# Cross-attention and soft mixture of experts: dispatch with an identity, token-major attention, another order in both stages

## The chip, the cores and the metric

The program runs on one core of a Trainium2 chip. The metric is the device time of one execution, in microseconds (us). TensorE multiplies (its products land in PSUM, eight banks of 512 float32 per partition), VectorE and ScalarE move and change data, GpSimd does plain tensor work, SyncE issues most transfers. Each engine works through its own list in order; semaphores join the lists.

## The reference, cut to what matters

```python
# x (32, 64, 256): 2048 tokens, 16 tiles of 128 tokens (2 sequences each); ctx (32, 64, 128)
q = layernorm(x) @ Wq; k, v = split(ctx @ Wkv)           # 32 heads of 8
q, k = rope(q, pos), rope(k, pos)
w = softmax(q . k / sqrt(8))                              # per head, 64 x 64
x = x + (w @ v) @ Wout + bout
xl = layernorm(layernorm(x)) * gamma + beta               # 16 experts, 128 slots each
logits = l2norm(xl) * scale . l2norm(mu)                  # token x 2048
dispatch = softmax over tokens; combine = softmax over the 2048 slots
slot_in = dispatch^T @ xl                                 # per sequence
h = gelu(slot_in @ W1 + b1)                               # 64 hidden
x = x + combine @ (h @ W2 + b2)
```

## The kernel before, in words

Everything stays in SBUF; a tile is 128 tokens. The first stage walks the 16 tiles through attention, the second through the experts. Both are software pipelines whose order is written out by hand, engine by engine: a `step(s)` of the first stage does the softmax of tile s, the rotary embedding of s + 1, the transposes of s + 2, the attend of s - 1 and the output projection of s - 2. Matmuls that want more than float32r precision are split in a high and a low part (`mm3`, lines 915 to 917, three passes). A plain float32 product is two passes in the profile, a transpose one.

First stage. TensorE projects q, k and v (`project_qk`, `project_v`), transposes q and k (`transpose_kq`, lines 948 to 951), forms the logits of the 32 heads in banks 0 to 3, with k masked by head so that pieces of 32 rows by 64 columns can be used (`logits`, line 965), transposes p (line 980), and attends (line 994). The attend has v as stationary operand, so the output comes transposed, and a second set of products with a matrix of ones, `hone`, gives the sums of p, repeated for each of the 8 dimensions of a head. VectorE takes maxima and subtracts (lines 677, 682), multiplies by cosine and sine (654, 656) into `ra` and `rb`, adds them (664), masks half of k (672), adds the residual and takes its statistics (702, 704), and divides (694, 696). ScalarE exponentiates (462), copies p transposed (466), v (479), q (483) and the other half of k (488), and casts x (493). GpSimd normalises x (347 to 353), and prepares mu, W1 and W2 with 2048-wide operations (378 to 407). The norms of mu's columns are summed on TensorE in steps 3 to 6 (1024) and spread over the partitions by a product of ones with a diagonal matrix between steps 7 and 8 (1085, 523).

Second stage, a tile: `expand` (xl @ W1, 12 passes), `transpose_e` (1127), the transposes of the next xl (1097), `dispatch` (1140), `slot_logits` of the next tile (24 passes of 512 columns), `combine` (1148, 1155) and `contract` (1161 and 24 passes of 256 columns). Dispatch computes e^T @ (xl @ W1), per expert, with both sequences of a tile in one product of 128 rows: the right side holds 65 columns for each sequence, with zeros in the other sequence's rows, and a column of ones that sums e over tokens. VectorE divides by that sum (842, 844), and ScalarE applies gelu (551). The exponent is line 539, the finish of a tile line 861.

## Time and profile before

| | us |
|---|---|
| median of 3 runs (range) | 567.08 (566.81 to 567.75) |
| span of the profiled execution | 560.9 |
| TensorE, VectorE, ScalarE, GpSimd busy | 501.4, 422.3, 290.3, 148.5 |
| second softmax starts | 37.94 |
| first, last finish of a tile in the second stage | 268.7, 558.1 |

The span runs from the first to the last instruction of one execution; the profile gives no other time for that execution, and the runs' median is 6.2 us above the span. A busy share is an average over both stages. The weight loads (PEld) overlap the passes (PE). The timelines count from the span's start; the end of a pass is modelled, so the rate of passes is best read from one start to the next.

### The profile page before, as it was taken

The numbers are of one execution on the slowest core, as the hardware profiler recorded it, in microseconds if no ns is written. First come the engines' busy times: TensorE is split into PE (matmuls) and PEld (weight loads), VectorE is DVE, ScalarE is ACT, GpSimd is POOL, SyncE is SP. The second block draws the span as 40 slices with busy tenths as digits, with TensorE's granted clock in tenths as the row PEclk, the third lists the DMA queues.
The fourth block names the chain that finished last, engine by engine and source line by source line (L and its number), as shares of the span: only waits on it lengthen the run. The fifth ranks groups of instructions, "written<-read, shape, count | busy, mean of one in ns | idle before, by whom it ended". The sixth has DMA issues, their size and how long they took to land.

```text
span 560.9 us, 14312 instructions
## 1 busy us (share of the span) xinstructions
PE 501.4 (89%) x5544; PEld 406.3 (72%) x5544; DVE 422.3 (75%) x823; ACT 290.3 (52%) x537; POOL 148.5 (26%) x248
## 2 busy tenths in 40 slices
PE   0676999987797878889999999999999999999997
PEld 0444666654565555668888898898889889888986
DVE  5788998896799999856866686686668668666854
ACT  1363656664354646635455635745563574556344
POOL 4329211518363832311211212111121211112100
PEclk9868999999698989999999999999999999999999
DMA  6500000006000200000000000000000000000000
GB/s 188 197 6 6 8 6 7 8 1 160 6 6 5 62 0 1 4 1 1 11 11 2 11 9 9 0 9 9 0 9 9 9 0 9 9 0 9 11 11 11
DMA packets 15665, 11.65 MB, mean 21 GB/s; under 512 B 7040, under 2 KB 15120, under 8 KB 15376
## 3 DMA queue, kind: packets, MB, share of 16 engines
q1 hardware_dynamic: 15632, 11.18, 6.7%
q8 instruction: 25, 0.41, 0.3%
q14 instruction: 8, 0.07, 0.0%
HBM read 9.08 MB, written 2.10 MB: 20 GB/s over the span
## 4 chain that ended last, share of the span: by engine, by line
PE 75%; DVE 16%; ACT 3%; issue 2%; SPq 1%; DMA 1%; POOL 0%; DVEq 0%; ACTq 0%
PE bank L915 13%; PE bank L917 12%; PE bank L916 12%; PE bank L1140 10%; PE bank L1155 6%; PE bank L1127 5%; DVE qkr L664 4%; PE bank L965 4%; PE bank L980 4%; PE bank L994 3%; DVE rc L694 3%; PE bank L1014 2%; DVE mx L677 2%; PE bank L1161 2%; DVE pb L682 2%
## 5 line engine op out<-in xcount | busy, mean ns | idle before, releaser
L462 ACT ACTIVATE pb<-pb 128x512 f32<-128x512 f32 x64 | 39.4, 632 | 64.2 <-DVE pb L682 64.2
L545 ACT COPY mu_raw<-bank 128x512 f32<-128x512 f32 x34 | 19.7, 588 | 98.4 <-PE bank L1127 98.4
L1140 PE MATMUL bank<-w_raw,eb 128*128 128x130 f32 x512 | 60.2, 275 | 1.0 <-DVE w_raw L815 0.9
L1140 PEld LDWEIGHTS bank<-w_raw,eb 128*128 128x128 f32 x512 | 58.5, 190 | 1.5 <-DVE w_raw L815 1.4
L551 ACT ACTIVATE pb<-pb 128x768 f32<-128x768 f32 (+1 forms) x48 | 37.1, 774 | 40.1 <-DVE pb L844 40.1
L915 PE MATMUL bank<-mun_h,xlT_l 128*128 128x512 f32 x128 | 51.9, 405 | 0.2 <-DVE xlT_l L806 0.2
L844 DVE TENSOR_TENSOR pb<-bank,rh 128x384 f32<-128x384 f32 x96 | 49.3, 513 | 3.3
L980 PEld LDWEIGHTS bank<-ident,pb 128*128 128x128 f32 x256 | 31.3, 156 | 27.7 <-issue 25.0
L980 PE MATMUL bank<-ident,pb 128*128 128x128 f32 x256 | 45.9, 309 | 5.8 <-ACT vb L479 3.6
L917 PE MATMUL bank<-mun_h,xlT_h 128*128 128x512 f32 x128 | 50.6, 395 | 0.0
L916 PE MATMUL bank<-mun_l,xlT_h 128*128 128x512 f32 x128 | 50.5, 395 | 0.0
L815 DVE TENSOR_TENSOR w_raw<-bank,mu_raw 64x512 f32<-64x512 f32 x64 | 44.1, 689 | 6.4 <-PE bank L917 4.9
L677 DVE TENSOR_REDUCE mx<-bank 128x8 f32<-128x512 f32 x64 | 41.0, 682 | 9.3 <-PE bank L965 9.2
L539 ACT ACTIVATE eb<-bank,nshift,rn 128x512 f32<-128x512 f32 x64 | 44.9, 777 | 3.2 <-PE bank L917 1.6
L965 PE MATMUL bank<-kT,qT 32*64 32x256 f32 x512 | 45.1, 443 | 0.0
L854 DVE TENSOR_TENSOR gT_l<-bank,gT_h 128x512 fp32r<-128x512 f32 x32 | 22.1, 692 | 26.8 <-ACT gT_h L556 26.8
L420 POOL TENSOR_TENSOR xc<-xc,mu_raw 128x256 f32<-128x256 f32 x16 | 11.8, 735 | 115.0 <-DVE xc L792 115.0
L334 POOL TENSOR_TENSOR sm<-sm,mhalf 128x1 f32<-128x1 f32 x16 | 8.8, 549 | 123.6 <-DVE sm L799 123.6
L682 DVE TENSOR_TENSOR pb<-bank,mx 128x512 f32<-128x512 f32 x64 | 40.9, 679 | 0.0
L466 ACT COPY pT<-bank 128x512 f32<-128x512 f32 x64 | 35.7, 594 | 7.9 <-PE bank L980 7.7
L850 DVE COPY esT<-bank 16x128 f32<-16x128 f32 x16 | 4.4, 278 | 45.8 <-PE bank L1148 45.8
L915 PE MATMUL bank<-w_h,gT_l 128*128 128x256 f32 x128 | 37.1, 290 | 0.0
(156 smaller groups left out, 1261.2 us busy)
## 6 DMA issues: line engine op xcount, KB each, us to landing
mu_raw<-in_L_ffn_mu SPq DMA_DIRECT2D x1, 2048.0 KB, 12.8
out<-w_raw SPq DMA_DIRECT2D x16, 128.0 KB, 1.7
xa<-in_x SPq DMA_DIRECT2D x1, 1536.0 KB, 8.4
ctile<-in_ctx SPq DMA_DIRECT2D x16, 64.0 KB, 1.9
w_raw<-in_L_ffn_W SPq DMA_DIRECT2D x2, 512.0 KB, 5.3
w_raw<-in_L_ffn_W SPq DMA_DIRECT2D x1, 1024.0 KB, 9.1
xa<-in_x SPq DMA_DIRECT2D x1, 512.0 KB, 3.6
mu_raw<-in_L_ffn_b SPq DMA_DIRECT2D x1, 512.0 KB, 3.1
```

The lines of the kernel that those rows point to most:

```text
L462: a.activation(pb[:, p, gr], pb[:, p, gr], ACT.Exp, scale=HD ** -0.5).then_inc(p_ready, 1)
L539: a.activation(eb[:, 4 * c:4 * c + 4, :].rearrange("p a b -> p (a b)"), bank[LB[c]][:], ACT.Exp, scale=rn[:, p:p + 1], bias=nshift[:]).the ...
L677: v.reduce_max(mx[:, gr, :], bank[gr][:].rearrange("p (h k) -> p h k", k=SEQ), AX.X)\
L682: v.tensor_tensor(pb[:, p, gr], bank[gr][:].rearrange("p (h k) -> p h k", k=SEQ), mx[:, gr, :].unsqueeze(2).broadcast_to([P, 8, SEQ]), ALU ...
L815: v.tensor_tensor(xw[rows, 8 * c:8 * c + 8, b * HC:b * HC + HID], bank[2 + c][rows].rearrange("p (e h) -> p e h", h=HID), b1b[rows, 8 * c: ...
L844: v.tensor_tensor(hb[:, e0:e0 + n], src[:, :, :, 0:HID], rh[:, e0:e0 + n, :].unsqueeze(3).broadcast_to([P, n, 2, HID]), ALU.mult).then_inc ...
L915: mm(o, a[1], b[0], start=first, stop=False)
L916: mm(o, a[0], b[1], start=False, stop=False)
L917: return mm(o, a[0], b[0], start=False, stop=last)
L965: m = mm(bank[g][cols, 256 * half:256 * half + 256].rearrange("p (j n) -> p j n", j=4), qT[rows, half, cols], kT[rows, half, :, cols], sta ...
L980: m = nc.tensor.transpose(bank[6 + gr % 2][:, i * P:(i + 1) * P], pb[:, p, gr, 2 * i:2 * i + 2, :].rearrange("p h k -> p (h k)"), ident[:])
L1140: m = mm(bank[HB[i % 3]][:, n * 2 * HC:(n + 1) * 2 * HC], eb[:, e, :], xw[:, e, :], start=True, stop=True)
```

## The change

In words, for what the diff below leaves out as well:

- Second stage: each expert's dispatch is two products, one for each sequence, on 64 rows each and into two neighbouring banks. Their right side is xl @ W1 + b1 and the ones (65 columns) beside a 64 x 64 identity, so that columns 65 to 128 hold e transposed; `transpose_e` is gone. ScalarE copies those columns to eT for each group of three experts, and only then VectorE divides that group. `xw_copy` adds b1 for both sequences at once. b2 and the sums of e are split in three float32r parts, and one pass replaces the float32 product. expand of s + 1 and the transposes of s + 2 come ahead of contract of s. The sums of e are taken a bank at a time. The LN statistics of later tiles move from the first stage into tiles 0, 4 and 8 of the second.
- First stage: the attend has p transposed as stationary operand and v as moving one, with 2 columns of ones for the sums, so the output is token-major with 32 sums; it is divided (`on`), transposed on TensorE (`transpose_o`) and copied by ScalarE (`oT`). The sine product stays in the bank, q, k and all transposes of tile s + 1 share bank 4, six scaled copies of k are ScalarE's and two heads' copies are VectorE's. The logits of all four row groups come together. The steps of TensorE and ScalarE are written out instead of looped over.
- mu's inverse norms go to DRAM and come back spread over the partitions by a transfer, and GpSimd reads them with a stride.
- Start: x of tile 0 has its own transfer and is normalised by VectorE; the weights are on ScalarE's queue; dummy transposes of the identity stand in TensorE's list.

```diff
+XC = HC + SEQ
+VC = 2 * HD + 2
...
+vb = sb("vb", P, 3, 2, HEADS // 2, VC)
...
-PER = BANK // (2 * HC)
+PER = BANK // XC
 HG = [range(i, min(i + PER, EXPERTS)) for i in range(0, EXPERTS, PER)]
 GG = [(HG[i][0], HG[min(i + 1, len(HG) - 1)][-1] + 1) for i in range(0, len(HG), 2)]
-NB = (6, 7, 5, 6)
-LB = (0, 1, 2, 5)
-HB = (4, 5, 3)
+LB = (2, 3, 0, 1)
+HB = (6, 0, 4)
...
+def pair(i, n):
+    b0 = HB[i % 3]
+    return psum[:, b0:b0 + 2, 0:n * XC].rearrange("p b (n c) -> p b n c", c=XC)
...
-    sp.dma_start(xa[:, 0:AHEAD, :], x_d[:, 0:AHEAD, :]).then_inc(x_loaded[0], 16)
+    sp.dma_start(xa[:, 0, :], x_d[:, 0, :]).then_inc(x_loaded[0], 16)
     load_ctx(0, 0)
-    sp.dma_start(wqkv_raw[:, 0:KD, :], Wq.rearrange("(k p) n -> p k n", p=P)).then_inc(wqkv_loaded, 16)
-    sp.dma_start(wqkv_raw[:, KD:KD + 2, :], Wkv.rearrange("p (k n) -> p k n", k=2)).then_inc(wqkv_loaded, 16)
-    sp.dma_start(posb[:], pos_d).then_inc(pos_loaded, 16)
+    sp.dma_start(xa[:, 1:AHEAD, :], x_d[:, 1:AHEAD, :]).then_inc(x_loaded[1], 16)
+    load_ctx(1, 1)
+    sp.wait_ge(wqkv_loaded, 32)
...
             load_ctx(i * 2 + p, p)
-    sp.wait_ge(rb_filled, 4)
+    load_ctx(10, 0)
+    sp.wait_ge(mur_ready, 1)
+    sp.dma_start(mur_d, mu_r[:, 1, :]).then_inc(mur_stored, 16)
+    sp.wait_ge(mur_stored, 16)
+    sp.dma_start(mu_rb, row(mur_d.rearrange("s e -> (s e)"), ES)).then_inc(rb_loaded, 16)
+    load_ctx(11, 1)
...
+        mu_k = mu_raw[:, k, :].rearrange("p (e s) -> p e s", s=SLOTS)
+        g.tensor_tensor(mu_k, mu_k, mu_rb.rearrange("p (s e) -> p e s", e=EXPERTS), ALU.mult)\
+            .then_inc(muscale_step, 1)
...
+    a.dma_start(posb[:], pos_d).then_inc(pos_loaded, 16)
+    a.dma_start(wqkv_raw[:, 0:KD, :], Wq.rearrange("(k p) n -> p k n", p=P)).then_inc(wqkv_loaded, 16)
+    a.dma_start(wqkv_raw[:, KD:KD + 2, :], Wkv.rearrange("p (k n) -> p k n", k=2)).then_inc(wqkv_loaded, 16)
...
+    def k1_copy(t, b=4, b0=4):
+        for half, j in ((1, 0), (1, 1), (1, 2), (1, 3), (0, 2), (0, 3)):
+            src = bank[b][:, DIM:DIM + P] if half else bank[b0][:, DIM + P:DIM + 2 * P]
+            a.activation(kT[:, half, j, :], src, ACT.Copy, scale=hmask[:, j:j + 1]).then_inc(k1_ready, 1)
...
+    def oT_copy(t):
+        act.wait_ge(oT_filled, t + 1)
+        wait(act, a_filled, t)
+        a.copy(oT[:], bank[5][:, 0:DIM]).then_inc(oT_ready, 1)
+    def step(s, p, before=True, after=True, out=True, ahead=True):
+        if before:
+            for gr in range(2):
+                pT_copy(s - 1, gr)
+        for gr in range(2):
+            exp_group(s, p, gr)
+        if out:
+            oT_copy(s - 2)
+        if before:
+            for gr in range(2, GROUPS):
+                pT_copy(s - 1, gr)
         if after:
-            v_copy(s + 1, 1 - p)
+            v_copy(s + 1)
             q_copy(s + 1)
+            k1_copy(s + 1)
             if ahead:
-                xT_high(s + 2)
-            k1_copy(s + 1)
-    act.wait_ge(consts_dve, 4)
-    xT_high(0)
...
+    def eT_copy(t):
+        for i, gr in enumerate(HG):
+            n, e0 = len(gr), gr[0]
+            act.wait_ge(h_filled, t * len(HG) + i + 1)
+            a.copy(eT[:, e0:e0 + n, :].rearrange("p n (b k) -> p b n k", b=2),
+                   pair(i, n)[:, :, :, HC:XC]).then_inc(eT_ready, 1)
...
-        v.tensor_tensor(rb[:], src, sinb[:, t, :].unsqueeze(1).broadcast_to([P, 64, 8]), ALU.mult)\
+        v.tensor_tensor(src, src, sinb[:, t, :].unsqueeze(1).broadcast_to([P, 64, 8]), ALU.mult)\
             .then_inc(ropeab_done, 1)
...
         dve.wait_ge(ropeab_done, t * 2 + 2)
+        rb = bank[4][:].rearrange("p (h c e) -> p (h c) e", c=4, e=2)
         for e in range(2):
             v.tensor_tensor(qkr[:].rearrange("p a (n e) -> p (a n) e", e=2)[:, :, e],
                             ra[:].rearrange("p h (c e) -> p (h c) e", e=2)[:, :, e],
-                            rb[:].rearrange("p h (c e) -> p (h c) e", e=2)[:, :, 1 - e],
+                            rb[:, :, 1 - e],
                             ALU.add).then_inc(qk_roped, 1)
...
-    def normalise(t):
+    def normalise(t, b=5):
         dve.wait_ge(o_filled, t + 1)
-        v.reciprocal(rc[:], bank[4][:, DIM:2 * DIM]).then_inc(rc_done, 1)
+        src = bank[b][:, 0:HEADS // 2 * VC].rearrange("p (q c) -> p q c", c=VC)
+        v.reciprocal(rc[:].rearrange("p (q j) -> p q j", j=2), src[:, :, 2 * HD:VC]).then_inc(rc_done, 1)
         dve.wait_ge(rc_done, t + 1)
-        v.tensor_tensor(oT[:], bank[4][:, 0:DIM], rc[:], ALU.mult).then_inc(oT_ready, 1)
...
+    def step(s, p, before=True, after=True, out=True, ahead=True, norms=False, stats=False):
         softmax(s, p, 0)
         if after:
             rope_products(s + 1)
+            rope_sums(s + 1)
+        if out:
+            residual(s - 2, stats=stats)
         if norms:
             dve.wait_ge(muss_ready, 1)
-            v.tensor_scalar(mu_r[:, 0, :], bank[5][:, DIM:DIM + EXPERTS], L2_EPS * L2_EPS, None, ALU.max)\
+            v.tensor_scalar(mu_r[:, 0, :], bank[5][:, BANK - EXPERTS:BANK], L2_EPS * L2_EPS, None, ALU.max)\
                 .then_inc(muss_clamped, 1)
         softmax(s, p, 2)
         if after:
-            rope_sums(s + 1)
-        if out:
-            residual(s - 2)
-        if after:
             k0_copy(s + 1)
-        if ahead:
-            xT_low(s + 2)
         if before:
             normalise(s - 1)
+        if ahead:
+            xT_low(s + 2, p)
...
+    def slot_sums(t, chunks=range(4)):
+        for c in chunks:
+            dve.wait_ge(e_ready, t * 4 + c + 1)
+            v.reduce_sum(es[:, 4 * c:4 * c + 4], eb[:, 4 * c:4 * c + 4, :], AX.X).then_inc(es_ready, 1)
...
+    def hidden(t):
         for i, gr in enumerate(HG):
-            if i == 3 and not last:
-                eT_copy(t, 3)
             n, e0 = len(gr), gr[0]
-            dve.wait_ge(h_filled, t * len(HG) + i + 1)
-            src = bank[HB[i % 3]][:, 0:n * 2 * HC].rearrange("p (n b c) -> p n b c", b=2, c=HC)
-            v.reciprocal(rh[:, e0:e0 + n, :], src[:, :, :, HID]).then_inc(rh_done, 1)
+            dve.wait_ge(eT_ready, t * len(HG) + i + 1)
+            src = pair(i, n)
+            v.reciprocal(rh[:, :, e0:e0 + n], src[:, :, :, HID]).then_inc(rh_done, 1)
             dve.wait_ge(rh_done, t * len(HG) + i + 1)
-            v.tensor_tensor(hb[:, e0:e0 + n], src[:, :, :, 0:HID],
-                            rh[:, e0:e0 + n, :].unsqueeze(3).broadcast_to([P, n, 2, HID]),
+            v.tensor_tensor(hb[:, e0:e0 + n].rearrange("p n b h -> p b n h"), src[:, :, :, 0:HID],
+                            rh[:, :, e0:e0 + n].unsqueeze(3).broadcast_to([P, 2, n, HID]),
                             ALU.mult).then_inc(hn_ready, 1)
...
             clamp(s + 1, 1 - p)
-        xw_copy(s)
-        if not last:
-            xlT_copy(s + 1)
-        hidden(s, last)
-        if not last:
-            eT_copy(s, 1)
+        hidden(s)
         if ahead:
             center(s + 2, p)
+        if stats:
+            batch_stats(stats)
+        if not last:
+            slot_sums(s + 1)
+        esT_copy(s)
         gT_low(s)
         if not last:
+            xw_copy(s + 1)
             sums(s + 1, 1 - p)
+        if ahead:
+            xlT_copy(s + 2)
         finish(s, p)
...
+    def keep_busy(n):
+        for _ in range(n):
+            nc.tensor.transpose(bank[5][:, 0:P], ident[:], ident[:])
...
+    def logits(t):
+        pe.wait_ge(q_ready, t + 1)
+        pe.wait_ge(k1_ready, t * 6 + 6)
+        pe.wait_ge(k0_ready, t + 1)
         wait(pe, sub_done, t * 4)
-        nc.tensor.transpose(bank[2][:, 0:P], qkr[:, 1, 0:P], ident[:]).then_inc(kq_filled, 1)
-        for k in range(KD):
-            nc.tensor.transpose(bank[3][:, k * P:(k + 1) * P], qkr[:, 0, k * P:(k + 1) * P], ident[:])
-        nc.tensor.transpose(bank[3][:, DIM:DIM + P], qkr[:, 1, P:2 * P], ident[:]).then_inc(kq_filled, 1)
...
-                if half and b:
-                    m.then_inc(s_filled, 1)
+        for half in range(2):
+            for b in range(2):
+                for g in range(GROUPS):
+                    rows, cols = slice(32 * g, 32 * g + 32), slice(64 * b, 64 * b + 64)
+                    m = mm(bank[g][cols, 256 * half:256 * half + 256].rearrange("p (j n) -> p j n", j=4),
+                           qT[rows, half, cols], kT[rows, half, :, cols], start=True, stop=True)
+                    if half and b:
+                        m.then_inc(s_filled, 1)
...
+    def attend(t, bo=5):
...
+        for q in range(HEADS // 2):
+            i = 4 * (q % 8 // 2) + 2 * (q // 8) + q % 2
             for b in range(2):
-                for r in range(2):
-                    for g in range(GROUPS):
-                        c = 256 * r + 32 * (half * GROUPS + g)
-                        product(half, r, g, vb[:, p, b].rearrange("p r c -> p (r c)")[:, c:c + 32],
-                                slice(64 * b, 64 * b + 64), half * P + b * 64)
-            for r in range(2):
-                for g in range(GROUPS):
-                    m = product(half, r, g, hone[:, r, :], slice(0, P), DIM + half * P)
+                rows = slice(64 * b, 64 * b + 64)
+                m = mm(bank[bo][rows, q * VC:(q + 1) * VC], pT[:, i, rows], vb[:, t % 3, b, q, :],
+                       start=True, stop=True)
         m.then_inc(o_filled, 1)
+    def transpose_o(t):
+        pe.wait_ge(on_ready, t + 1)
+        wait(pe, x1_ready, t)
+        for k in range(KD):
+            m = nc.tensor.transpose(bank[5][:, k * P:(k + 1) * P], on[:, k * P:(k + 1) * P], ident[:])
+        m.then_inc(oT_filled, 1)
...
-        if before:
-            transpose_p(s - 1, 1 - p, 1, more=after)
-        logits(s, 0, 1)
-        if before:
-            transpose_p(s - 1, 1 - p, 2)
+            for gr in range(2):
+                transpose_p(s - 1, 1 - p, gr, more=after)
         if after and before:
-            project_qk(s + 1)
-        logits(s, 2, 0)
+            project_qk(s + 1, 1 - p)
         if norms is not None:
             mu_sums(s, norms)
+        if out:
+            transpose_o(s - 2)
         if before:
-            transpose_p(s - 1, 1 - p, 3)
-        logits(s, 2, 1)
-        if norms == 3:
-            pe.wait_ge(muss_clamped, 1)
+            for gr in range(2, GROUPS):
+                transpose_p(s - 1, 1 - p, gr)
         if out:
             for k in range(KD):
                 project_out(s - 2, k)
         if after:
-            project_v(s + 1)
-            if before:
-                attend(s - 1, 1 - p)
+            project_v(s + 1, 1 - p)
             transpose_kq(s + 1)
             if ahead:
                 transpose_x(s + 2, p)
+        if norms == 3:
+            pe.wait_ge(muss_clamped, 1)
+        if before:
+            attend(s - 1, 5 if after else 4)
+    keep_busy(24)
     transpose_x(0, 0)
+    keep_busy(8)
     pe.wait_ge(wqkv_ready, 1)
-    project_qk(0)
-    project_v(0)
+    project_qk(0, 0)
+    project_v(0, 0)
+    keep_busy(6)
     transpose_x(1, 1)
-    transpose_kq(0)
-    project_qk(1)
+    transpose_kq(0, 3, 2)
+    project_qk(1, 1)
...
+    def dispatch(t, last, first=False):
+        pe.wait_ge(xw_ready, t * 2 + 2)
         for i, gr in enumerate(HG):
-            if i == 0:
+            if i == 1:
+                pe.wait_ge(e_ready, t * 4 + 4)
+                if not last:
+                    pe.wait_ge(xlT_ready, t + 2)
+            if i == 2:
                 wait(pe, yo_ready, t)
+                if first:
+                    pe.wait_ge(x1_ready, TILES)
             if i >= 3:
                 pe.wait_ge(hn_ready, t * len(HG) + i - 2)
             for n, e in enumerate(gr):
-                m = mm(bank[HB[i % 3]][:, n * 2 * HC:(n + 1) * 2 * HC], eb[:, e, :], xw[:, e, :],
-                       start=True, stop=True)
+                for b in range(2):
+                    rows = slice(64 * b, 64 * b + 64)
+                    m = mm(bank[HB[i % 3] + b][:, n * XC:(n + 1) * XC], eb[rows, e, :], xw[rows, e, :],
+                           start=True, stop=True)
             m.then_inc(h_filled, 1)
...
+    def ffn_step(s, p, last=False, ahead=True, first=False):
+        dispatch(s, last, first)
         if not last:
             slot_logits(s + 1)
-        combine(s, last)
+        combine(s)
+        if not last:
+            expand(s + 1)
+        if ahead:
+            transpose_xl(s + 2, p)
         contract(s)
```

## Rows read from the trace of the kernel before

**Rows 1.** The page's first part: busy us, share of the span, instructions.
```profile
PE 501.4 (89%) x5544; PEld 406.3 (72%) x5544; DVE 422.3 (75%) x823; ACT 290.3 (52%) x537; POOL 148.5 (26%) x248
```

**Rows 2.** Windows: stretch, length, busy PE, PEld, DVE, ACT, POOL, clock, DMA share, GB/s.
```profile
0.00:38.00 38.00, 16.10 (x102) 11.73 (x103) 26.39 (x78) 13.47 (x31) 11.18 (x27) 0.84 0.45 144
109.38:120.84 11.46, 10.60 (x175) 7.16 (x167) 10.69 (x19) 7.21 (x19) 4.46 (x5) 1.00 0.01 3
120.84:143.40 22.56, 13.96 (x179) 8.59 (x175) 16.67 (x20) 10.89 (x27) 14.97 (x10) 0.96 0.42 100
227.40:268.75 41.35, 37.58 (x449) 30.48 (x448) 27.87 (x54) 19.80 (x33) 7.52 (x20) 1.00 0.01 2
425.45:445.06 19.61, 19.61 (x179) 17.22 (x178) 13.51 (x30) 10.43 (x15) 3.08 (x9) 1.00 0.02 7
```

**Rows 3.** Timeline of VectorE, one attention step: start, us, instruction.
```profile
112.06 1.75 DVE L694 RECIPROCAL rc<-bank 128x256 f32<-128x256 f32 x1
114.18 1.28 DVE L677 TENSOR_REDUCE mx<-bank 128x8 f32<-128x512 f32 x2
120.16 0.76 DVE L664 TENSOR_TENSOR qkr<-ra,rb 128x256 f32<-128x256 f32 x2
```

**Rows 4.** Groups by line (first), then timelines in the long step.
```profile
L664 DVE TENSOR_TENSOR qkr<-ra,rb 128x256 f32<-128x256 f32 x32 | 30.0, 984 | 0.1
132.03 4.56 POOL L396 TENSOR_TENSOR mu_raw<-mu_raw,eb 128x2048 f32<-128x2048 f32 x1
133.20 0.68 DVE L654 TENSOR_TENSOR ra<-bank,cosb 128x512 f32<-128x512 f32 x1
136.79 6.66 DVE L664 TENSOR_TENSOR qkr<-ra,rb 128x256 f32<-128x256 f32 x2
```

**Rows 5.** Timeline of ScalarE in an attention step.
```profile
116.09 1.23 ACT L462 ACTIVATE pb<-pb 128x512 f32<-128x512 f32 x2 [2.53 <-DVE pb L682]
121.05 1.11 ACT L479 COPY vb<-bank 64x128 f32<-64x128 f32 x4
122.83 1.16 ACT L488 ACTIVATE kT<-bank,hmask 128x128 f32<-128x128 f32 x4
```

**Rows 6.** Timeline of TensorE in an attention step.
```profile
67.03 0.66 PE L965 MATMUL bank<-kT,qT 32*64 32x256 f32 x8
67.62 1.05 PE L1024 MATMUL bank<-ones,eb 128*128 128x1 f32 x8
69.69 1.13 PE L1014 MATMUL bank<-wo,oT 128*128 128x256 f32 x4
```

**Rows 7.** Timeline of TensorE, second stage; last row: groups, 425.45 to 445.06.
```profile
419.98 2.09 PE L1155 MATMUL bank<-mu_raw,pb 128*64 128x64 f32 x64
421.99 0.69 PE L1161 MATMUL bank<-b2s,esT 16*128 16x256 f32 x2
428.25 1.91 PE L1127 MATMUL bank<-ident,eb 128*128 128x128 f32 x16
430.21 3.75 PE L1140 MATMUL bank<-w_raw,eb 128*128 128x130 f32 x32
L1140 PEld LDWEIGHTS bank<-w_raw,eb 128*128 128x128 f32 x32 | 3.7, 190 | 0.0
```

**Rows 8.** Groups by line of VectorE, second stage, 425.45 to 445.06.
```profile
L844 DVE TENSOR_TENSOR pb<-bank,rh 128x384 f32<-128x384 f32 (+1 forms) x6 | 3.1, 514 | 0.2
L842 DVE RECIPROCAL rh<-bank 128x6 f32<-128x6 f32 (+1 forms) x6 | 1.1, 180 | 0.0
L815 DVE TENSOR_TENSOR w_raw<-bank,mu_raw 64x512 f32<-64x512 f32 x4 | 2.8, 688 | 0.5 <-PE bank L917 0.4
```

**Rows 9.** Timelines of VectorE; first and last start of line 861.
```profile
37.94 1.28 DVE L677 TENSOR_REDUCE mx<-bank 128x8 f32<-128x512 f32 x2
L861 DVE SCALAR_TENSOR_TENSOR w_raw<-bank,rs,xa x16: 482/484/485, 268.7 to 558.1; 128x256 f32<-128x256 f32 x16
543.64 0.48 DVE L861 SCALAR_TENSOR_TENSOR w_raw<-bank,rs,xa 128x256 f32<-128x256 f32 x1
```

523 lines of the change are left out of this document (254 added, 269 removed).

## The prediction

> **What bounds the kernel now.** I read the page's busy times first: TensorE is busy 89% of a 560.9 us span and VectorE 75% [rows 1]. Those are averages over two stages with different limits, so next I cut the span by tile [rows 2]. In the second stage a tile takes 19.61 us and TensorE is busy for 19.61 of them, at full clock, VectorE for 13.5, ScalarE for 10.4: TensorE alone binds. In the first stage a quiet tile takes 11.46 us with VectorE busy 10.69, TensorE 10.60 and ScalarE 7.21: there VectorE's order binds, and the others follow at its heels. The stretch after it, 120.84 to 143.40, is one tile too, and takes 22.56 us; the first 38 us hold TensorE at clock 0.84 and 16.1 us of work.
>
> The timelines say why. In an attention step VectorE spends 1.75 us on one 256-wide reciprocal, 2.4 us on each half of the softmax (two maxima, 1.28 with the overlap, and two subtractions as long) and 0.76 on the two rotary sums [rows 3]. In the long tile the two rotary sums take 6.66 us instead of 0.76, while GpSimd works on 2048-wide tensors; a rotary product, which reads a bank, keeps its 0.68 beside the same kind of GpSimd work [rows 4]. So VectorE is held up where both operands lie in SBUF. All 32 sums take 30.0 us where 16 x 0.76 is 12.2: some 17 us of the stage are stretched sums. Of the long tile's 11.1 us beyond its neighbour 5.9 are its sums, and the other 5 TensorE's broadcast of the mu norms, for which everything waits.
>
> **The second stage, per tile.** Removed: 16 transposes of e, 1.74 us (18 with two of xl from 428.25 to 430.21, 0.109 each) [rows 7], since dispatch now multiplies by an identity too and leaves the transpose beside its result. The b2 product falls from 0.63 us (0.69 with its tail) to one pass of the kind that contract uses for the same 256 columns, which come at 0.11, so 0.52 less. Slot logits, expand, combine and contract keep their instructions. Dispatch itself was 32 passes of 130 columns, 3.75 us with the last one's tail and 3.5 without, 0.109 each. It becomes 64 passes of 129 columns, each on 64 rows, in two row halves with a bank of their own. If the halves run side by side it stays at 64 x 0.109 / 2 = 3.5; if they take turns, 64 x 0.109 = 7.0; if each weight load shows, 64 x 0.190 = 12.2. Nothing of before uses a half of 64 rows. The nearest row is the attention logits, which use 32-row by 64-column pieces: 8 passes of 256 columns in 0.59 us (67.03 to the next start), 0.074 each, where the output projection's four passes of 256 columns take 1.13 [rows 6]. So pieces do run side by side, and I take 3.5.
>
> The page "TensorE: Matmul & The Clock Gate" of the Trainium skill, section "LDWEIGHTS (loading the stationary operand)", speaks against this: a load costs by its columns and not its rows, some 107 ns for 128. The combine's 64-column loads come every 32 ns here [rows 7], below its 53, so loads of two column pieces do overlap; no row here shows it for two row pieces. By that rule without overlap 64 loads are an estimated 6.8 us; the section "Key Properties" of its page "TensorEngine Tiling (Array Packing)" has tiles load in parallel.
>
> Dispatch gets a longer chain for its banks: group 3 waits until ScalarE has copied group 0's transposes (128x384, which I price at 0.5, between the 128x512 exponent at 0.6 and nothing) and VectorE has divided (0.18 and 0.51, 0.56 for a full group) [rows 8]. That is 0.66 + 0.1 + 0.5 + 0.1 + 0.75 = 2.1 us against 1.97 when TensorE would come to group 3, and VectorE's 0.69 a group is a little over TensorE's 0.66: about 0.3 us of stall, 3.8 in all. Bounds 0 and 1. Sum: 19.61 - 1.74 - 0.52 + 0.3 = 17.65; I take 17.6.
>
> What hides the rest: ScalarE gets some 2.7 us of copies for 1.2 removed, 12 of 17.6. VectorE loses two copies (1.36) and half of the x W1 additions (they work on 128 instead of 64 partitions: 2.85 to 1.4), gains some 0.9 in split sums and casts: about 12. The exponents of tile s+1 then end 11.8 us after dispatch of s starts, the gT casts at 12.9, VectorE's low parts at 14.0, and contract starts at 14.6: 0.6 us of cover, the smallest of the step. Dispatch's other new waits end early: the exponents 5.8 us before it and the cast of the next xl under 1 us before it, both asked for at group 1, and the finish of the tile before 0.6 us after it starts, while group 2 comes at 1.3. The statistics moved here (2.6 us, in three tiles) fall where VectorE waits for exponents. The three b2 loads, GpSimd's extra deviations and the new identity fill lie in idle queues, at nothing.
>
> 14 intervals, from 268.7 to 543.64 [rows 9], are 274.9 us now and become 14 x 17.6 = 246.4. The last tile, 14.4 us, has no slot logits; its own chain (dispatch 3.8, gelus to 7.9, combine 9.4, casts 10.7, half of contract, finish) gives 13.
>
> **The first stage, per tile.** VectorE: reciprocal of 32 instead of 256 values, 1.75 to 0.35 (0.18 for 6 values in the second stage, the rest by length); statistics gone, 0.35; k0 two heads of four, 0.25 less. Its work falls from 10.7 to about 8.7. In place in the bank the second rotary product could cost 0.60 (as now) to 1.2; I take 0.60. The rotary sums read a bank, and by the row above are no longer stretched: 0.7.
> ScalarE: six scaled copies of k for four, 1.65 (0.27 each [rows 5]), and a copy of oT, 0.35, make 8.4 of 7.2. TensorE: the attend is 64 passes of 18 columns with 64-column weights, priced like the combine, 64 x 0.032 = 2.0 [rows 7], as now; above, like logits, 4.7, of which 1 is covered. Logits of all four row groups at once: between 1.2 (twice the pieces in flight) and 2.4 (4 x 0.59); I take 1.3.
>
> So no engine is full, and the chain through all of them sets the step: q and k of tile s+1 must be in place before its logits. Times from the start of logits(s): logits and semaphore 1.4; first half of softmax, 2.4, to 3.8; its second exponent 4.5 [rows 5]; oT copy 4.85; output projection 1.1 [rows 6] and values, three passes of 0.12, 0.36, with semaphores to 6.5; v copies 1.1 to 7.6; q 0.3, k 1.65 to 9.55; k0, which now waits for the last k copy, to 9.95, and the division of tile s-1 and the low part of s+2 queued behind it come to 11.2, 1.1 us into the next step, which asks for them at 3.5 and 2.4. Beside it VectorE: products and sums to 5.7, residual, second half of softmax to 8.9. TensorE: 16 p transposes and the q and k projections, under 3.5 at these rates, fit in 1.3 to 4.85. 10.05 by hand; such a hand schedule leaves out small waits, I take 10.4 (bounds 10.0 and 11.5, the step of now). In four steps the mu sums (1.0 [rows 6]) lie on that chain: +0.9 each.
> The mu broadcast leaves TensorE: a store and a 1 MB load. TensorE and ScalarE wait for neither; GpSimd waits for the load before tile 10's norm, some 10 us of DMA against two steps. mu's strided read on GpSimd may cost twice its 4.6 us twice: it has over 30 us of slack before slot logits. The SP queue stands at the store, with context 10 already issued. Unrolled steps only add code to fetch.
>
> **The start.** The second softmax starts at 37.94 now [rows 9]. Tile 0 comes by its own load, is normalised by VectorE without waiting for the scale, weights come on ScalarE's queue, and 8 statistics and their moments (3.8 us) move out of these 38 us. kq(1) has its own bank and doesn't wait for the first softmax. VectorE has 26.4 us of work before 38 [rows 2], 22.6 then, and I count 8.8 of waits left of 11.6, the longest for GpSimd's norm of tile 1: 31.4. Bounds 29 and 37. The 62 dummy transposes before that lie where TensorE waits, and keep its clock up, now 0.84: at most a microsecond either way.
>
> **Sum.** Softmax of tile 15 starts at 31.4 + 14 x 10.4 + 4 x 0.9 = 180.6 (227.4 now). From there to the first finish 41.35 us [rows 2], now 41: the same TensorE work less 2.3, a little more waiting. Then 246.4 + 13 + 2.8 after the last finish (558.1 to 560.9) [rows 9]: 483.8 of span, against 560.9. The runs' median, 567.08, is 6.2 above that span; the profiled execution's own time isn't given otherwise. 483.8 + 6.2 = **490**.
>
> **Rivals.**
> - *The halves of dispatch take turns* (7.0 for 3.8): 16 x 3.2 = 51 more, 541. For it: TensorE's order is kept, and a pass of 128-column weights never came faster than 0.109 in any row. Against: the logits' 0.074. The Trainium skill's rule on loads, above, would end here too.
> - *The attention step stays at 11.5*, since the chain leaves the engine that got faster: rotary in place is slow, or logits 2.4. 14 x 1.1 = 15 more, 505.
> - *The sums are still stretched* though one operand is in a bank, so that the edit doesn't do what it says: the 17 us stay, 507. Against it the 0.68 of [rows 4].
> - *Slower than before*: the 64 weight loads of dispatch are exposed, since a pass of 129 columns on half of the rows can't cover the load of the other half. Price 64 x 0.190 = 12.2, 8.4 more a tile, 134 in all: 624. It decides once a pass costs over (3.8 + 77/16) / 64 = 0.134 us. For it: the load's own 0.190. Against: in every row now loads hide behind passes.
>
> **How the numbers follow.** Forecast 0.58, turns 0.20, step at 11.5 0.11, stretched sums 0.05, exposed loads 0.06. The forecast's own range is 472 to 512: 10.0 and 17.4 with 39 between the stages give 478, 11.2 and 18.0 with the start at 33 give 509. To leave out no more than 2 in 10 the range must reach the halves in turns: 472 to 546. Faster by over 0.2% (about what a measurement tells from no change) 0.93, within it 0.01, slower 0.06.
>
> **What would show it.** Second-stage finishes 17.6 us apart, TensorE busy nearly all of it, and dispatch's passes 0.055 apart; 0.109 is the first rival, more the last. Attention residuals 10.4 apart, VectorE waiting for ScalarE's k copies, rotary sums of 0.45 at their longest. Second softmax near 31. It is wrong if finishes are further apart than 18, or if a gap behind dispatch's bank waits or contract's low parts exceeds half a microsecond.

## The result and the profile after

The changed kernel takes 492.36 us (median of 4 runs, 491.32 to 493.89) against 567.41 us (566.81 to 569.53) for the kernel before on the same chip: a ratio of 0.867, 95% interval 0.863 to 0.870. A second series gave 492.44 us and 0.868 (0.865 to 0.871). The profiled execution took 491.93 us with a span of 490.0. The prediction was 490. Two runs of the kernel before that stand beside some of the experiments (571.71 and 572.36 us) were over 1.5% above its fastest and are left out of all ratios and ranges here.

The page's first part, beside [rows 1]:

```profile
PE 448.7 (92%) x5358; PEld 390.5 (80%) x5358; DVE 350.1 (71%) x891; ACT 312.7 (64%) x643; POOL 150.0 (31%) x269
```

TensorE lost 53 us of work, VectorE 72, ScalarE gained 22. The stretches that answer to [rows 2] come next: the start up to the second softmax, a quiet attention step, an attention step with a fallen clock, a tile of the second stage, and the last tile from finish to finish. Columns: stretch, length, busy time (instructions) by engine, granted clock, DMA share, GB/s.

```profile
0.00:31.72 31.72, 18.90 (x168) 15.72 (x169) 23.21 (x76) 13.21 (x33) 18.62 (x42) 0.94 0.55 173
120.64:130.61 9.97, 8.55 (x139) 7.58 (x138) 8.83 (x17) 7.95 (x21) 9.83 (x7) 1.00 0.03 8
160.48:171.39 10.91, 9.65 (x138) 8.24 (x137) 9.79 (x25) 7.77 (x21) 1.94 (x6) 0.84 0.01 2
344.76:362.93 18.17, 18.11 (x193) 15.66 (x192) 13.79 (x43) 11.39 (x19) 5.07 (x15) 1.00 0.02 8
471.92:487.16 15.24, 12.06 (x154) 11.20 (x154) 6.00 (x16) 7.11 (x12) 0.00 (x0) 0.78 0.03 10
```

The second-stage tile went from 19.61 to 18.17 us and is still TensorE's alone (18.11 busy). A quiet attention step went from 11.46 to 9.97, and there no engine is full: VectorE 8.83, TensorE 8.55, ScalarE 7.95. The long step of 22.56 us is gone: from 120.64 to 130.61 GpSimd is busy for 9.8 us, most of it on 2048-wide tensors, and the step is no longer than others. In the third row TensorE ran partly at its lower level (1.2 GHz); the logits took 2.02 us there instead of 1.12. But this step is also the one in which VectorE works out the moments of the first tiles' statistics (9.79 busy), and the same step took 10.58 at clock 1.00 in the run with other groups below, so only some 0.3 of its excess is the clock's. One other attention step of this execution has a fallen clock, the first one with mu sums (46.78 to 58.55, 11.77 us, clock 0.86).

The chain in the quiet attention step (second row), in three timelines (start, us, instruction, idle time before it and what ended it). TensorE, from the attend on:

```profile
121.53 2.05 PE L1085 MATMUL psum<-vb,pT 128*64 128x18 f32 x64
124.68 1.12 PE L1053 MATMUL psum<-kT,qT 32*64 32x256 f32 x32 [1.10 <-DVE kT L730]
```

ScalarE: v, q and six k copies.

```profile
120.88 1.13 ACT L518 COPY vb<-psum 64x128 f32<-64x128 f32 x4 [0.60 <-PE psum L1004]
122.03 0.37 ACT L523 COPY qT<-psum 128x256 f32<-128x256 f32 x1
122.30 1.67 ACT L529 ACTIVATE kT<-psum,hmask 128x128 f32<-128x128 f32 x6
```

VectorE: the second softmax of the run, then k0 and the reciprocal, which [rows 3] has at 1.75.

```profile
31.72 1.29 DVE L735 TENSOR_REDUCE mx<-psum 128x8 f32<-128x512 f32 x2 [1.85 <-PE psum L1053]
124.00 0.42 DVE L730 TENSOR_TENSOR kT<-psum,hmask 128x256 f32<-128x256 f32 x1 [0.55 <-ACT kT L529]
124.34 0.35 DVE L753 RECIPROCAL rc<-psum 128x32 f32<-128x32 f32 x1
```

VectorE's groups by line for the two rotary lines (busy, mean ns of one, idle before).

```profile
L721 DVE TENSOR_TENSOR qkr<-ra,psum 128x256 f32<-128x256 f32 x32 | 12.1, 422 | 0.9
L712 DVE TENSOR_TENSOR psum<-psum,sinb 128x512 f32<-128x512 f32 x16 | 11.0, 689 | 0.0
```

One line of the second stage by itself, its finishes: count, shortest, median and longest ns, first and last start.

```profile
L926 DVE SCALAR_TENSOR_TENSOR w_raw<-psum,rs,xa x16: 482/482/484, 217.7 to 487.2; 128x256 f32<-128x256 f32 x16
```

In the attention step TensorE waits 1.10 us for VectorE's k0, VectorE 0.55 for ScalarE's k, and ScalarE had been waiting for the values: the chain of the prediction, link by link. The 32 rotary sums take 12.1 us where [rows 4] has 30.0, and the product in place in the bank costs 0.689, not more than the 0.680 of one that writes elsewhere.

Dispatch in TensorE's timeline (with the pass that follows, and the last tile's waits), and ScalarE's copies of its transposes, one for each group of three experts:

```profile
344.76 4.22 PE L1213 MATMUL psum<-w_raw,eb 64*128 64x129 f32 x64
348.92 0.50 PE L1002 MATMUL psum<-mun_h,xlT_l 128*128 128x512 f32 x1
...
471.81 4.22 PE L1213 MATMUL psum<-w_raw,eb 64*128 64x129 f32 x64
477.67 0.30 PE L1220 MATMUL psum<-ident,es 128*128 128x128 f32 x1 [1.65 <-DVE pb L907]
479.41 3.68 PE L1228 MATMUL psum<-mu_raw,pb 128*64 128x64 f32 x64 [1.44 <-ACT pb L597]
```

```profile
345.75 0.48 ACT L591 COPY mu_raw<-psum 128x384 f32<-128x384 f32 x1 [5.60 <-PE psum L1213]
346.42 0.48 ACT L591 COPY mu_raw<-psum 128x384 f32<-128x384 f32 x1 [0.19 <-PE psum L1213]
347.09 0.48 ACT L591 COPY mu_raw<-psum 128x384 f32<-128x384 f32 x1 [0.19 <-PE psum L1213]
348.09 0.48 ACT L591 COPY mu_raw<-psum 128x384 f32<-128x384 f32 x1 [0.52 <-PE psum L1213]
```

Groups end 0.67 us apart, 12 passes each: 0.056 a pass. Taken one by one, the passes start in pairs, two within 0.007 us and the next pair 0.11 later. The fourth group ends 1.00 after the third, 0.33 more than the others: the gap between two pairs is 0.33 there instead of 0.11, so some 0.23 is the wait for the bank, and the pair behind it is followed after 0.21 instead of 0.11, another 0.10. The whole of dispatch is 348.92 - 344.76 = 4.16 us.

### The profile page after: what moved, and what is told of

It reads as the page before. It is cut to its first block, busy times and chain, and to the rows that moved or that the text cites. A ratio compares the mean times of both kernels' runs of the same rounds, so it can differ in the third digit from the quotient of the medians.

```text
span 490.0 us, 13729 instructions
## 1 busy us (share of the span) xinstructions
PE 448.7 (92%) x5358; PEld 390.5 (80%) x5358; DVE 350.1 (71%) x891; ACT 312.7 (64%) x643; POOL 150.0 (31%) x269
## 4 chain that ended last, share of the span: by engine, by line
PE 69%; DVE 13%; ACT 12%; issue 5%; POOL 1%; DVEq 0%; POOLq 0%; ACTq 0%
PE psum L1002 14%; PE psum L1003 13%; PE psum L1004 13%; PE psum L1213 9%; PE psum L1228 7%; ACT kT L529 4%; PE psum L1053 4%; PE psum L1101 3%; DVE mx L735 3%; PE psum L1068 2%; ACT vb L518 2%; DVE pb L740 2%; DVE pb L907 2%; ACT mu_raw L591 2%; ACT pb L504 2%
## 5 line engine op out<-in xcount | busy, mean ns | idle before, releaser
L591 ACT COPY mu_raw<-psum 128x384 f32<-128x384 f32 x96 | 41.0, 445 | 104.3 <-PE psum L1213 104.3
L885 DVE TENSOR_REDUCE es<-eb 128x4 f32<-128x512 f32 x64 | 43.1, 686 | 56.4 <-ACT eb L583 56.4
L1213 PE MATMUL psum<-w_raw,eb 64*128 64x129 f32 x1024 | 66.6, 279 | 1.0
L1213 PEld LDWEIGHTS psum<-w_raw,eb 64*128 64x128 f32 x1024 | 60.4, 187 | 6.3 <-DVE pb L907 4.1
L1002 PE MATMUL psum<-mun_h,xlT_l 128*128 128x512 f32 x128 | 52.6, 411 | 0.2 <-DVE xlT_l L871 0.2
L907 DVE TENSOR_TENSOR pb<-psum,rh 128x384 f32<-128x384 f32 x96 | 49.2, 513 | 3.3
L1003 PE MATMUL psum<-mun_l,xlT_h 128*128 128x512 f32 x128 | 50.7, 396 | 0.0
L1004 PE MATMUL psum<-mun_h,xlT_h 128*128 128x512 f32 x128 | 50.7, 396 | 0.0
L583 ACT ACTIVATE eb<-psum,nshift,rn 128x512 f32<-128x512 f32 x64 | 44.9, 776 | 2.3 <-PE psum L1004 2.0
L735 DVE TENSOR_REDUCE mx<-psum 128x8 f32<-128x512 f32 x64 | 41.0, 681 | 4.1 <-PE psum L1053 3.9
L740 DVE TENSOR_TENSOR pb<-psum,mx 128x512 f32<-128x512 f32 x64 | 40.9, 679 | 0.0
```

What stands on the lines that cost most here:

```text
L583: a.activation(eb[:, 4 * c:4 * c + 4, :].rearrange("p a b -> p (a b)"), bank[LB[c]][:], ACT.Exp, scale=rn[:, p:p + 1], bias=nshift[:]).the ...
L591: a.copy(eT[:, e0:e0 + n, :].rearrange("p n (b k) -> p b n k", b=2), pair(i, n)[:, :, :, HC:XC]).then_inc(eT_ready, 1)
L735: v.reduce_max(mx[:, gr, :], bank[gr][:].rearrange("p (h k) -> p h k", k=SEQ), AX.X)\
L740: v.tensor_tensor(pb[:, p, gr], bank[gr][:].rearrange("p (h k) -> p h k", k=SEQ), mx[:, gr, :].unsqueeze(2).broadcast_to([P, 8, SEQ]), ALU ...
L907: v.tensor_tensor(hb[:, e0:e0 + n].rearrange("p n b h -> p b n h"), src[:, :, :, 0:HID], rh[:, :, e0:e0 + n].unsqueeze(3).broadcast_to([P, ...
L1002: mm(o, a[1], b[0], start=first, stop=False)
```

## The experiments

Ratios are to the kernel before, on the same chip; in brackets stand the range of the runs behind a time and the 95% interval behind a ratio. The unaltered changed kernel ran again only beside the two combinations and the run with four k copies and dummies, on one chip; the other runs are set against it by their ratio (0.867 is its own) and by the steps in their traces.

**Row halves one after the other.** Each group's three products of rows 0 to 63 come first, then its three of rows 64 to 127.

```
-                    for n, e in enumerate(gr):
-                        for b in range(2):
-                            rows = slice(64 * b, 64 * b + 64)
-                            m = mm(bank[HB[i % 3] + b]..., eb[rows, e, :], xw[rows, e, :], ...)
+                    for n, e in enumerate(gr):
+                        m = half_product(i, n, e, 0)
+                    for n, e in enumerate(gr):
+                        m = half_product(i, n, e, 1)
```

> The changed kernel, but each group of three experts first issues the products of the one sequence's 64 rows and then those of the other's, where the changed kernel alternates. Same passes, same banks, same result. Theory (two row halves run side by side only where they follow each other closely in TensorE's list): a pass falls back from 0.056 us to 0.109 in a row, dispatch goes from 4.2 to about 7 us a tile, the second stage's step from 18.2 to about 21, and the time to about 492 + 16 x 2.9 = 538. Rival (the halves have lists of their own and the order does not matter, or the pass became cheaper because only half of the rows hold data): dispatch stays at 4.2 and the time at 492.

One run, 504.13 us, span 502.1; second-stage step 18.78. Both expectations miss. (A single run fixes the time only roughly, and three of its attention steps had a fallen clock; the argument rests on the steps.) The windows of its dispatch line alone (busy time and number of passes in flight, PE and PEld) show how:

```profile
351.85:351.90 0.05, 0.05 (x1) 0.05 (x1) 1.00 0.00 0
352.10:352.15 0.05, 0.05 (x4) 0.05 (x3) 1.00 0.00 0
353.10:353.15 0.05, 0.05 (x6) 0.05 (x4) 1.00 0.00 0
```

The same windows of the changed kernel begin with two in flight:

```profile
344.80:344.85 0.05, 0.05 (x2) 0.05 (x2) 1.00 0.00 0
345.35:345.40 0.05, 0.05 (x6) 0.05 (x4) 1.00 0.00 0
```

With six passes of one half ahead of six of the other there is one pass in flight at first, then as many as in the changed kernel, and its groups also end 0.67 us apart. Taken one by one, its first passes start singly (351.80, 352.01) and from 352.45 on in pairs, a pair every 0.11, as in the changed kernel. A 256-column pass of this type on all rows takes 0.20 (output projection, four from 129.31 to 130.09), so 129 columns alone can't take 0.056. And a pass that had become cheaper because only half of the rows hold data would start every 0.056 and not in twos: the two halves run beside each other, though in program order they lie six passes apart. The lag of one half costs 0.31 us up to the end of the first group (1.30 after the start, 0.99 in the changed kernel) and 0.31 around the bank wait (1.31 for 1.00): 0.6 us a tile, not 3.3. So the first rival of the prediction, halves that take turns, didn't come about even in the order that invites it most.

**The second rotary product in SBUF.** The sine product goes to a tile in SBUF instead of staying in its bank, so the sums have both operands in SBUF again.

```
-                v.tensor_tensor(src, src, sinb[:, t, :]...
+                v.tensor_tensor(rb_sb[:], src, sinb[:, t, :]...
-                rb = bank[4][:].rearrange("p (h c e) -> p (h c) e", c=4, e=2)
+                rb = rb_sb[:].rearrange("p h (c e) -> p (h c) e", e=2)
```

> The changed kernel with the sine product written to an SBUF tile, as before the change, instead of back into its bank; the rotary sums then read two SBUF operands. Theory (VectorE is held up by GpSimd's 2048-wide operations where both operands are in SBUF): the 32 sums take over 25 us in all instead of 12.1, single ones 3 to 5 us long beside GpSimd's long operations, and the time rises by 10 to 18 us, to 502 to 510; the step in quiet stretches stays 9.96. Rival (the stretching came from another thing that the change also moved, as GpSimd's order): sums 12, time within 1 us of 492.

512.29 us (509.36 to 514.79), ratio 0.902 (0.897 to 0.908), two above the range expected. The sums in VectorE's groups by line, two pairs of them in its timeline, and GpSimd's timeline beside the first pair:

```profile
L722 DVE TENSOR_TENSOR qkr<-ra,rb_sb 128x256 f32<-128x256 f32 x32 | 27.3, 894 | 0.9
```

```profile
112.15 5.95 DVE L722 TENSOR_TENSOR qkr<-ra,rb_sb 128x256 f32<-128x256 f32 x2
130.66 0.76 DVE L722 TENSOR_TENSOR qkr<-ra,rb_sb 128x256 f32<-128x256 f32 x2
```

```profile
110.22 5.57 POOL L431 TENSOR_TENSOR mu_raw<-mu_raw,eb 128x2048 f32<-128x2048 f32 x1
115.86 1.97 POOL L382 CAST mun_h<-mu_raw 128x2048 fp32r<-128x2048 f32 x1
```

The sums go from 12.1 to 27.3 us, the first finish from 217.7 to 240.5, and the second stage keeps its 18.17. The pair that starts at 112.15 ends at 118.10, right behind GpSimd's two operations (115.79 and 117.83); the pair at 130.66, with GpSimd idle, takes 0.76. So the place of one operand is worth 20 us, more than the 15 of lengthened sums: the steps behind also lose clock (0.59 in the one from 118 to 131; 0.937 over the run against 0.979). The Trainium skill, page "SBUF — State Buffer", section "Who interferes with whom", has the rule: a VectorE instruction with two SBUF inputs contends with a GpSimd instruction that reads SBUF, the shared ports being under an exclusive lock, and one with at most one SBUF input (outside the 2-port modes) does not. The trace agrees on both sides: 4.6 us at most for one sum here, 0.44 in the changed kernel.

**Groups of 2, 3, 3, 3, 3, 2 experts.**

```
-        HG = [range(i, min(i + PER, EXPERTS)) for i in range(0, EXPERTS, PER)]
+        HG = [range(a, b) for a, b in zip((0, 2, 5, 8, 11, 14), (2, 5, 8, 11, 14, 16))]
```

> The changed kernel with dispatch's experts in groups of 2, 3, 3, 3, 3, 2 instead of five of 3 and one of 1. Theory (dispatch's 4.16 us instead of 3.6 are the wait for group 0's banks, whose chain ScalarE copy, reciprocal, product is longer than two groups of passes): the chain of a group of two is shorter by 0.2 to 0.3, the wait falls from about 0.35 to 0.1, the step from 18.17 to 17.9, the time by 4 us to 488. Rival (the extra 0.5 us is the cost of the 64-row form itself, as changes of the array's division): no change in step or time.

490.19 us (486.87 to 492.79), ratio 0.864 (0.858 to 0.871), not to be told from the changed kernel's; step 18.13. ScalarE's copies in one of its tiles:

```profile
347.30 0.48 ACT L591 COPY mu_raw<-psum 128x384 f32<-128x384 f32 x1 [0.19 <-PE psum L1213]
348.05 0.48 ACT L591 COPY mu_raw<-psum 128x384 f32<-128x384 f32 x1 [0.27 <-PE psum L1213]
348.97 0.84 ACT L591 COPY mu_raw<-psum 128x384 f32<-128x384 f32 x2 [0.45 <-PE psum L1213]
```

The delay of 0.33 of the fourth group became 0.08 for the fourth and 0.25 for the fifth. It isn't an effect of the first group: copy, reciprocal and division of a group follow each other on its banks and take longer than the other two groups give. The theory missed; 0.04 us a tile is what is left of 0.3. (The profile's span of 488.9 is 1.1 shorter than the changed kernel's, but its last tile, 13.96 instead of 15.24, gives more than that, and there it is the clock that came back sooner.)

**No dummy transposes.** All 62 are taken out of the first tiles.

```
-            keep_busy(24)
             transpose_x(0, 0)
-            keep_busy(8)
...
-            keep_busy(6)
...
-            keep_busy(24)
```

> The changed kernel without its 62 dummy transposes. Theory (they only keep the clock up and lie where TensorE waits for others): granted clock of the first 32 us falls from 0.94 to about 0.8, the projections of tiles 0 and 1 and the logits take up to 1 us longer each where they lie on the chain, and the time rises by 1 to 2 us. Rival (the dummies are in the way, transposes of x queued behind them): the time falls by up to 1 us. A second rival (they matter more, a cold start carries on into later steps): 5 us or more slower.

494.23 us (493.0 to 495.37), ratio 0.873 (0.868 to 0.878). The second softmax starts at 32.59 instead of 31.72, the first finish comes at 218.6 instead of 217.7. Over its first 32 us:

```profile
0.00:32.00 32.00, 11.76 (x105) 9.20 (x105) 23.19 (x75) 13.27 (x33) 18.52 (x42) 0.90 0.54 171
```

The clock is 0.90 there against 0.93 with them, not the 0.8 expected. Profiles of five executions with the dummies and the same start have the second softmax between 31.34 and 32.31, so 32.59 is hardly outside them. If the dummies are worth anything, it is about a microsecond, and neither these starts nor the intervals separate that from nothing.

**The kernel before, with mu's norms spread by DMA** instead of by products with a diagonal.

```
+            sp.dma_start(mur_d, mu_r[:, 1, :]).then_inc(mur_stored, 16)
+            sp.wait_ge(mur_stored, 16)
+            sp.dma_start(mu_rb, row(...)).then_inc(rb_loaded, 16)
...
-                mm(bank[NB[c]][:], ones[:], diag[:, 4 * c:4 * c + 4, :]...).then_inc(rb_filled, 1)
-            pe.wait_ge(rb_ready, 4)
```

> The kernel before with one part of the change alone: the norms of mu are spread over the partitions by a store and a load of 1 MB instead of by four TensorE products with a diagonal on GpSimd; every operation of the steps and the second stage is the old one. Theory (the broadcast was 5 of the 11.1 us by which the long step of 22.56 us exceeded its neighbour, the stretched sums the other 5.9): the long step falls to some 17.5, the sums of the rotation stay at about 30 us, the run comes to 562. Rival 1 (the broadcast was hidden behind the stretched sums, which hold VectorE at the same time): 567, no change. Rival 2 (GpSimd's diagonal was itself what stretched the sums): both 11 go, 556, and the sums fall under 25 us.

562.53 us (562.39 to 562.66) against 562.85 to 571.04 for the kernel before on this chip, ratio 0.987 (0.982 to 0.993). The kernel before scatters by more than the effect, so the steps decide. Its long step, and a later step in which the clock fell:

```profile
123.56:139.18 15.62, 10.68 (x171) 7.18 (x167) 14.88 (x20) 8.33 (x23) 13.99 (x6) 0.95 0.58 140
168.56:182.85 14.29, 14.16 (x167) 10.13 (x167) 10.93 (x19) 6.41 (x14) 1.87 (x3) 0.65 0.02 5
```

The long step is 6.9 shorter (22.54 to 15.62), more than the 5 of the theory. But 1.6 of it is that its own two sums take 5.05 instead of 6.66; a later pair takes 1.0 more, and all 32 take 29.5, about as long as before. That leaves 5.3 for the broadcast, the theory's 5. The step from 168.56 is 2.7 longer than its like in the kernel before (11.61 at clock 0.85), and the stretch from 38 us to the first residual is 2.7 longer too, at clock 0.79 instead of 0.89. So the span, 560.6, is no shorter than the 560.9 of the kernel before, whose profile is that of a short execution. The run fits the theory's 562 with the clock's share in it, which the theory didn't have.

**Values copied last.** ScalarE's next q and k no longer stand behind v.

```
                 if after:
-                    v_copy(s + 1)
                     q_copy(s + 1)
                     k1_copy(s + 1)
+                    v_copy(s + 1)
```

> The changed kernel with one order changed: ScalarE copies q and k of the next tile before it copies v. Theory (the attention step of about 10 us is set by the chain through all engines: half softmax, exponent, output projection, ScalarE's v, q and k copies, VectorE's k0, logits): the copy of v, 1.13 us with its start, leaves the chain and its 12 projection passes stay, so a step gets about 0.7 shorter where no other engine is full: 15 steps, 8 to 10 us, 483. Rival (VectorE, busy 8.8 of 10, or TensorE, 8.5, takes over at once, and the values product late behind the copy holds the attend): under 2 us, 491.

483.16 us (482.73 to 484.72), ratio 0.849 (0.844 to 0.854). One of its steps in the windows, and the logits in its timeline:

```profile
116.52:125.87 9.35, 8.55 (x139) 7.58 (x138) 8.75 (x17) 7.91 (x21) 9.19 (x8) 1.00 0.03 9
```

```profile
119.92 1.12 PE L1053 MATMUL psum<-kT,qT 32*64 32x256 f32 x32 [0.46 <-DVE kT L730]
```

Every engine has the work of 9.97 us in 9.35; TensorE's wait fell from 1.10 to 0.46. That shows the chain to be what set the step, and ScalarE's order a link of it. Of the 9.1 us by which the span is shorter (490.0 to 480.9) some 6 are the steps. Another 2.7 are clock: the first step with mu sums kept 1.00 (10.21 instead of 11.77), and in the last tile it came back sooner (14.14 instead of 15.24).

**Four k copies.** ScalarE copies four parts of k, VectorE makes k0 for all four heads.

```
-                for half, j in ((1, 0), (1, 1), (1, 2), (1, 3), (0, 2), (0, 3)):
+                for half, j in ((1, 0), (1, 1), (1, 2), (1, 3)):
...
-                v.tensor_tensor(kT[:, 0, 0:2], ...
+                v.tensor_tensor(kT[:, 0], ...
```

> The changed kernel with the k copies shared out otherwise: ScalarE makes four (all heads of the second half), VectorE all four heads of the first half in one operation. It tells how much of the step hangs on ScalarE's part of the chain. Theory of the chain: two copies of 0.27 leave it and VectorE's one grows by about 0.25, so 0.3 a step less, 4 to 5 us in all, 488. Rival (VectorE binds the step by its busy time of 8.8): 0.25 a step more, 4 us, 496.

492.06 us (491.51 to 497.02), ratio 0.866 (0.859 to 0.873): nothing won. But the steps are of two kinds:

```profile
109.79:119.48 9.69, 8.52 (x139) 7.55 (x138) 9.10 (x17) 7.43 (x19) 9.47 (x6) 1.00 0.12 35
119.48:130.27 10.79, 9.94 (x139) 8.74 (x137) 9.11 (x18) 7.40 (x19) 10.23 (x7) 0.84 0.03 8
130.27:139.91 9.64, 8.69 (x139) 7.58 (x138) 9.07 (x19) 7.43 (x19) 6.18 (x5) 1.00 0.03 9
139.91:150.69 10.78, 9.93 (x139) 8.74 (x137) 9.10 (x17) 7.44 (x19) 9.52 (x5) 0.84 0.48 87
```

At clock 1.00 a step takes 9.66, the 0.3 of the chain theory; every other one has part of its work at half clock and takes 10.8 (five of the nine from 89 to 182). The same instructions, so the shorter chain was paid back by the clock.

**Four k copies and dummies ahead of the logits**, to see whether that was the clock's doing.

```
+                wait(pe, sub_done, t * 4)
+                if t >= 3:
+                    for _ in range(6):
+                        nc.tensor.transpose(bank[0][:, 0:P], ident[:], ident[:])
                 pe.wait_ge(q_ready, t + 1)
...
-                wait(pe, sub_done, t * 4)
```

> The kernel with four k copies, and ahead of each step's wait for q and k six transposes that nobody reads, from step 3 on. With four copies alone the wait ahead of the logits fell from 1.10 to 0.85 and a step at clock 1.00 from 9.96 to 9.66, but every other step had a clock of 0.84 and took 10.75, so nothing was won. Theory (those 1.1 us are the clock's doing): with TensorE running through part of the wait the clock stays at 1.00, all steps take 9.7, and the run comes to 492 - 4 = 487 to 488. Rival (the long steps come from something else in them, such as GpSimd's work beside VectorE, and the clock is only low by its side): every other step still takes 10.7 and the run 492; or the dummies come late, behind sub_done, and delay the logits by up to 0.4 a step: 494.

484.91 us (483.15 to 486.48), ratio 0.854 (0.850 to 0.858). Two of its steps in the windows, and in the timeline the dummies between attend and logits:

```profile
117.13:126.75 9.62, 9.28 (x145) 8.12 (x144) 9.10 (x17) 7.42 (x19) 9.40 (x8) 1.00 0.03 9
126.75:136.34 9.59, 9.25 (x145) 8.09 (x144) 9.10 (x17) 7.42 (x19) 8.51 (x6) 1.00 0.03 9
```

```profile
129.62 0.87 PE L1048 MATMUL psum<-ident 128*128 128x128 f32 x6
130.43 1.12 PE L1056 MATMUL psum<-kT,qT 32*64 32x256 f32 x32
```

From 76.5 to 175.7 every step has clock 1.00, and none of 10.8 is left. GpSimd is busy for 9.40 and 8.51 in these steps, within the 6.18 to 10.23 of the run before, so the rival falls. The first step with mu sums and the last tile kept more of the clock as well (10.47 for 12.01, 14.18 for 15.31).

**Dummies in the last tile**, 30 behind dispatch.

```
                 dispatch(s, last, first)
+                if last:
+                    for _ in range(30):
+                        nc.tensor.transpose(bank[2][:, 0:P], ident[:], ident[:])
```

> The changed kernel with 30 transposes that nobody reads behind the last tile's dispatch, where TensorE waits 1.65 and 1.44 us and its clock is then granted at half of full speed, so that the combine takes 3.68 us instead of 2.08. Theory (the last tile is 2.2 us longer than forecast since the clock falls after those waits): the clock stays at full speed, combine takes 2.1 and contract is unstretched, last tile 13.3 instead of 15.24, 490.5. Rival (the clock falls all the same, or the dummies delay the combine by as much): 492 to 494.

491.29 us (489.1 to 492.05), ratio 0.861 (0.856 to 0.866). The last tile in the windows, and the dummies and the combine in its timeline:

```profile
474.00:487.19 13.19, 12.93 (x184) 11.99 (x184) 6.01 (x16) 7.11 (x12) 0.00 (x0) 1.00 0.04 12
```

```profile
478.04 3.50 PE L1245 MATMUL psum<-ident 128*128 128x128 f32 x30
481.58 2.08 PE L1228 MATMUL psum<-mu_raw,pb 128*64 128x64 f32 x64
```

13.19 instead of 15.24, near the prediction's 13. The profiled execution as a whole kept its 490.0 of span, since three attention steps fell to a clock of 0.84 or 0.85 that kept 1.00 in the profile of the changed kernel; the gain stands in the tile and hardly in the median.

**The changed kernel again, and the combinations.**

> The changed kernel once more, unaltered, as the base for the two combinations on the same chip. Every theory: 492, between 490 and 494; second-stage step 18.17, quiet attention step 9.95. Where an attention step takes some 11 instead, TensorE's granted clock in it is about 0.84 instead of 1.00.

492.44 us (491.62 to 494.15), as expected. From 79 to 171 one step of the profiled execution has a clock of 0.84 (160.26 to 171.06, 10.80 us, the one with the moments); the others have 1.00, also the last one with mu sums (11.41).

> Three edits at once: v copied behind q and k, dispatch in groups of 2, 3, 3, 3, 3, 2 experts, 30 dummy transposes behind the last dispatch. If their gains add up (8.0 from the order, 0.04 a step and some tenths in the last tile from the groups, 2.05 from the last tile's clock): 483.2 - 0.6 - 1.0 = 481.5, attention step 9.34, second-stage step 18.13, last tile 13.1. (With the order alone the last tile took 14.13, so of the 2.05 only 1 is left.) Rival (the dummies only move where the clock falls): 483.

481.88 us (480.49 to 483.21), ratio 0.849 (0.846 to 0.852): the best version, 10.6 us (2.1%) below the changed kernel on the same chip. Steps 9.32 and 18.14, last tile 13.15: the gains add up, to within 0.4 of the 481.5 expected.

> The three edits of the run before, and ScalarE makes four k copies, VectorE all of k0. Chain theory: another 0.25 a step goes from TensorE's wait ahead of the logits (0.46 there with the order changed), the step falls to 9.1, 15 x 0.25 = 3.7 less: 478. Rival 1 (VectorE, 8.75 + 0.25 = 9.0 busy, with its own waits of 0.3, binds): step 9.3 to 9.4, no gain, 481.5. Rival 2 (the granted clock falls in every other step, as it did with the four copies alone): such steps take 10.2 and the run 485.

488.00 us (485.07 to 488.46), ratio 0.859 (0.856 to 0.862). A step at full clock, and one that isn't:

```profile
109.05:118.63 9.58, 8.52 (x139) 7.56 (x138) 9.01 (x17) 7.41 (x19) 9.44 (x3) 1.00 0.19 62
118.63:129.36 10.73, 10.01 (x139) 8.77 (x137) 9.06 (x17) 7.33 (x19) 10.51 (x9) 0.84 0.03 8
```

Both rivals hold and the theory falls: with q and k first VectorE's order binds (8.75 of 9.32 busy in the run before, 9.01 of 9.58 here), so its longer k0 adds its 0.25 in full; and four of the seven steps from 109 to 180 fell to clock 0.84 on top. The six dummies together with the new order were not tried.

## Why the prediction was right

**The span adds up, with misses both ways.** Forecast 483.8, measured 490.0: start +0.3, attention steps -4.1, 14 second-stage intervals +7.8, last tile +2.2; the stretches between the stages (40.9) and after the last finish (2.8) as forecast. The step from span to time was wrong: I added 6.2, taken from the median of the kernel before less its profiled span, but in every later run of either kernel span and time lie some 1.8 to 2.2 apart (490.0 and 491.93). The profiled execution of before was a short one of its kernel, some 562.8 us by that difference. So 490 against 492 is +6.2 and -4.3: two misses of opposite sign, and that the number came so close is luck; the mechanism of each part is what holds. (By its own terms the low end of the forecast's range is 480 and not 478, which changes nothing.)

Where the 71 us of span went, profile against profile: the start 6.2, the attention stage 44.3 (189.5 to 145.1), between the stages 0.5, the 14 intervals of the second stage 20.7, and the last tile cost 0.8 (14.43 to 15.24). Of the 44.3 the sums and the broadcast are sized by the experiments above; the token-major attend with its short reciprocal, the moved statistics and the changes at the start weren't run apart.

**Dispatch: right mechanism, 0.36 too short.** The halves run side by side at 0.056 a pass, and the bank wait is 0.23 where 0.3 was forecast. What I left out is that the passes in flight have to climb from two to six again (the windows above): 0.10 behind the first pair, 0.10 behind the bank wait, and 0.10 more on the way out, since the slot logits start 0.20 behind the last pair. Two small stalls further on and rounding make the rest. The 130-column passes of [rows 7] on all rows came straight behind the transposes at 0.11 each. The Trainium skill, page "TensorEngine Tiling (Array Packing)", section "Key Properties", states that a change of tiling mode drains the engine; the trace agrees in so far as two of these three losses lie where the 64-row form is entered and left, but the third, behind the bank wait, comes without such a change. With the first experiment, neither order of the halves loses the overlap. The rival with exposed loads would have needed 0.134 a pass.

**The rest of the second-stage step**, 18.17 for 17.6: dispatch +0.36, b2 saved 0.41 and not 0.52 (0.21 from its start to contract's first pass), expand 2.91 for 2.80, since its first pass behind the combine takes 0.34 instead of 0.23, slot logits +0.04; the two transposes of xl, now in other company, gave 0.09 back. Each change of pass kind costs about 0.1, and the new order has more of them. None of the new waits of ScalarE and VectorE shows: TensorE is busy 18.11 of 18.17.

**Attention: the hand schedule was right and the allowance on it wrong.** 10.05 by hand, 9.96 measured, 10.4 taken. The four steps with mu sums were to take 11.3 each. Two took 10.3: the sums, 0.81 from their start to the next pass, use up the 0.32 that TensorE otherwise waits for oT, while its wait for k0 stays 1.10, and the step gets 0.3 longer, not 0.9. The first took 11.77 at clock 0.86. The fourth took 11.41 at full clock: VectorE's statistics of the later tiles (83.98 to 85.89) stand ahead of its second pair of maxima, and TensorE waits for oT.

```profile
89.34 1.13 PE L1101 MATMUL psum<-wo,oT 128*128 128x256 f32 x4 [1.06 <-ACT oT L538]
```

Over the stage that gives 145.1 us for the forecast's 149.2, the -4.1, with two clock falls in it, of some 1.5 and 0.3 us, that the forecast didn't have. The experiment with v copied last shows the chain by shortening it: the copies' 1.13 leave, 0.62 is won, and from there VectorE's order binds (in the best version it is idle for 0.57 of 9.32). The rival "step stays at 11.5" fell, rotary in place at 0.689 and logits at 1.05 for 32 passes.

**Sums and broadcast: right, both sized by experiment.** The stretched sums are worth 20 us on today's kernel, the clock lost behind them included, where I had 17; the broadcast is 5.3 on the old one (5 forecast).

**The start.** The second softmax at 31.72 for 31.4. The dummy transposes were put at "at most a microsecond either way", and no more than that showed when they were removed.

**The last tile: the wrong step.** 15.24 for 13: I priced its chain at full clock. It has two waits, 1.65 and 1.44 us, that no tile before has, since there slot logits fill them; the clock in it is 0.78, and the combine took 3.68 for 2.08. With TensorE kept running the same chain took 13.19. What the fall costs varies: without dummies there the last tile took 13.96 to 15.37 us in the other profiles that have dispatch as here or in the other groups.

**What would show it wrong.** I had named finishes more than 18 us apart, and they came at 18.17. By that bound the step's sum was wrong though the mechanism was not: it was a bound of 0.4 us on a sum of seven terms. The other signs came as named: passes 0.056 apart, residuals 9.97, rotary sums of 0.44 at their longest, and no gap over half a microsecond in a tile but the last.

## What to carry to other kernels

When no engine is full in a step, look for the chain through all of them and ask which instruction on it stands behind one that nobody waits for: moving one ScalarE copy behind those that are waited for was worth some 6 us of steps, and the clock gave 3 more; fewer copies on the chain were worth nothing until the clock was held. When a cut at TensorE's input brings nothing, compare the granted clock of neighbouring steps before looking for a new wait. And a VectorE operation beside a busy GpSimd should find one of its operands in a bank.

## What the runs showed that was not expected

- Products on two row halves overlap even when six passes of one half are issued ahead of six of the other: 0.67 us for 12 either way once both run, 0.6 us lost a tile.
- With a wait of 0.85 us ahead of the logits (four k copies) the clock of every other attention step was 0.84, at a price of 1.1 us. With the longer wait of 1.10 one step in nine had it in both profiled executions of the changed kernel, and two to four in those of four other runs whose attention code is the same (halves in turn, other groups, no dummies, dummies in the last tile). Six transposes in the wait, 0.87 us, held it at 1.00 throughout. What decides which steps fall stays open.
- GpSimd's product of mu with a strided second operand takes 5.6 us where the plain one took 4.56 [rows 4]; twice was feared.
